# A twelve-stage decoder on one core: layer norms by one-pass moments (BN_STATS, BN_AGGR), scaled and transposed sequence by sequence

## The reference

```python
def _layernorm(x, axis=-1, eps=1e-05):
    m = jnp.mean(x, axis=axis, keepdims=True)
    v = jnp.var(x, axis=axis, keepdims=True)
    return (x - m) / jnp.sqrt(v + eps)

x = x + _L0_attn_ref(_layernorm(x, axis=-1), ...)
x = x + _L0_xattn_ref(_layernorm(x, axis=-1), ...)
x = x + _L0_ffn_ref(_layernorm(x, axis=-1), ...)
...
x = x + _L3_ffn_ref(_layernorm(x, axis=-1), ...)
```

## Time and profile before

| | |
|---|---|
| median of 3 runs | 1576.84 us (1575.34 to 1582.71) |
| the profiled execution | 1576.1 us, of which the span from the first to the last instruction is 1574.2 us |
| busy in the span | PE 1247.6 us (79%), DVE 902.8 us (57%), ACT 730.8 us (46%), POOL 325.2 us (21%) |
| mean granted TensorE clock | 0.857 of full speed |

### The profile page before, as it was taken

How to read it: one execution, slowest core, us unless ns; L and a number is a source line. 1 busy time by engine, 2 the same in 40 slices (tenths; PEclk the granted TensorE clock), 3 DMA queues, 4 the chain that set the end, 5 groups by cost and what they waited for, 6 DMA issues and landing times. The chain is left out here.

```text
span 1574.2 us, 24800 instructions
## 1 busy us (share of the span) xinstructions
PE 1247.6 (79%) x9007; PEld 814.7 (52%) x9008; DVE 902.8 (57%) x1989; ACT 730.8 (46%) x1316; POOL 325.2 (21%) x360
## 2 busy tenths in 40 slices
PE   5999797357697997487776874769789979797998
PEld 2788364136455564144653651755544434364776
DVE  3688473765666445686678568445634455474211
ACT  2344363341265323477568554436566633363442
POOL 0222200003220002346356251022000034300000
PEclk9899698565788997786997997688989989598999
DMA  6000000020000000000000000015036910000000
GB/s 262 1 1 0 1 2 1 0 83 1 0 1 2 0 1 1 0 1 1 1 1 1 1 1 1 2 72 228 2 78 124 202 31 1 0 2 2 1 1 14
DMA packets 15200, 44.28 MB, mean 28 GB/s; under 512 B 1872, under 2 KB 4976, under 8 KB 14448
## 3 DMA queue, kind: packets, MB, share of 16 engines
q1 hardware_dynamic: 15088, 42.80, 9.4%
HBM read 42.01 MB, written 0.79 MB: 27 GB/s over the span
## 5 line engine op out<-in xcount | busy, mean ns | idle before, releaser
L745 DVE TENSOR_REDUCE L_xattn_top<-banks 128x4 f32<-128x512 f32 x128 | 80.6, 671 | 54.9 <-PE banks L603 54.9
L750 DVE TENSOR_TENSOR L_xattn_p<-banks,L_xattn_top 128x512 f32<-128x512 f32 x128 | 82.5, 686 | 4.8
L700 ACT ACTIVATE L_xattn_p<-L_xattn_p 128x512 f32<-128x512 f32 x128 | 75.8, 630 | 18.1 <-DVE L_xattn_p L750 18.1
L708 ACT ACTIVATE L_xattn_pT<-banks 128x512 f32<-128x512 f32 x128 | 69.7, 595 | 20.1 <-PE banks L616 20.1
L603 PE MATMUL banks<-L_xattn_ks,L_xattn_qT 32*128 32x512 f32 x256 | 76.6, 702 | 1.6 <-ACT L_xattn_qT L689 1.6
L492 PE MATMUL banks<-w_const,h 128*128 128x128 f32 x96 | 24.0, 407 | 66.1 <-DVE h L487 66.1
L1277 DVE TENSOR_TENSOR L_ffn_a<-L_ffn_a,L_ffn_share 128x512 f32<-128x512 f32 x64 | 39.9, 687 | 60.1 <-DMA L_ffn_share<-L_ffn_shares 57.6
L616 PE MATMUL banks<-w_const,L_xattn_p 128*128 128x128 f32 x512 | 69.5, 278 | 5.2 <-ACT L_xattn_p L700 5.2
L476 POOL MEMSET norm_power<- 128x8 f32 x12 | 1.3, 105 | 344.7 <-POOLq L79 322.7
L1189 PE MATMUL banks<-L_ffn_a,region_a 128*128 128x512 f32 x136 | 67.5, 601 | 5.2 <-DVE L_ffn_a L1277 5.2
L1520 ACT ACTIVATE L_ffn_aT<-banks,L_ffn_shift 128x512 f32<-128x512 f32 x64 | 43.3, 687 | 58.9 <-PE banks L1470 57.3
(11 more groups left out here) (518 smaller groups left out, 3187.2 us busy)
## 6 DMA issues: line engine op xcount, KB each, us to landing
L_ffn_share<-L_ffn_shares SPq DMA_DIRECT2D x32, 512.0 KB, 10.2
region_b<-in_L_ffn SPq DMA_DIRECT2D x1, 6216.0 KB, 29.8
region_a<-in_L_ffn SPq DMA_DIRECT2D x1, 4416.0 KB, 14.6
region_b<-in_L_attn SPq DMA_DIRECT2D x1, 3150.5 KB, 10.2
region_a<-in_L_ffn SPq DMA_DIRECT2D x1, 3080.5 KB, 21.8
region_b<-in_L_attn SPq DMA_DIRECT2D x1, 1633.5 KB, 10.5
region_b<-in_L_xattn SPq DMA_DIRECT2D x1, 835.0 KB, 11.3
w_tables<-in_tables SPq DMA_DIRECT2D x1, 832.0 KB, 14.2
```

What stands on the lines that cost most here:

```text
L700: nc.scalar.activation(p[:, m % 4, :], p[:, m % 4, :], ACT.Exp, scale=scale).then_inc(exped, 1)
L708: nc.scalar.activation(pT[:, n % 2, 2 * (P % 2) + e, :], tps[e][:], ACT.Copy).then_inc(pT_kept, 1)
L745: nc.vector.tensor_reduce(top[:, i, :], rows_of(score[i][:], 4), X, ALU.max)
L750: nc.vector.tensor_tensor(rows_of(p[:, i, :], 4), rows_of(score[i][:], 4), bc(top[:, i, :], 2, T), ALU.subtract).then_inc(centered, 1)
```

## The change

`Norm` is rewritten; the calls around it follow.

- `center` and `variance` become one step, `take_moments`: four BN_STATS, one per sequence, each reading 128 elements per partition and writing six; a drain; four BN_AGGR, each reading those six and writing the mean and the variance; a drain; one addition of 1e-5 over the four variances.
- `square` is gone from ACT, and with it the tile of squares.
- `scale` reads `x` again and subtracts the mean and multiplies by the reciprocal root in one TENSOR_SCALAR per sequence, with both as per-partition scalars. Each adds one to `h_ready`.
- `turn` waits once per sequence instead of once per half.
- The constant -0.5 is written once at the program's start instead of once per stage.

DVE's instructions per norm go from 12 to 26, ACT's from 4 to 2. Everything else, the order of the calls and all other waits, stays.

```diff
-    def center(self, dve, half):
-        nc, g, b = self.nc, self.g, slice(4 * half, 4 * half + 4)
-        nc.vector.tensor_reduce(self.total[:, b], g.x[:, b, :], X, ALU.add)
-        dve.drain()
-        nc.vector.tensor_scalar(self.mean[:, b], self.total[:, b], 1.0 / D, None, ALU.mult)
-        dve.drain()
-        nc.vector.tensor_tensor(g.h[:, b, :], g.x[:, b, :], bc(self.mean[:, b], 2, D),
-                                ALU.subtract).then_inc(self.centered, 1)
-
-    def square(self, act, half):
+    def take_moments(self, dve, half, eps=1e-5):
+        nc, g = self.nc, self.g
+        for n in range(4 * half, 4 * half + 4):
+            nc.vector.bn_stats(self.stats[:, n, :], g.x[:, n, :])
+        dve.drain()
+        for n in range(4 * half, 4 * half + 4):
+            nc.vector.bn_aggr(self.moments[:, n, :], self.stats[:, n, :])
+        dve.drain()
         b = slice(4 * half, 4 * half + 4)
-        act.wait_ge(self.centered, half + 1)
-        self.nc.scalar.activation(self.sq[:, b, :], self.g.h[:, b, :], ACT.Square).then_inc(self.squared, 1)
-
-    def variance(self, dve, half, eps=1e-5):
-        nc, b = self.nc, slice(4 * half, 4 * half + 4)
-        dve.wait_ge(self.squared, half + 1)
-        nc.vector.tensor_reduce(self.sumsq[:, b], self.sq[:, b, :], X, ALU.add)
-        dve.drain()
-        nc.vector.tensor_scalar(self.var[:, b], self.sumsq[:, b], 1.0 / D, eps, ALU.mult, ALU.add).then_inc(self.var_ready, 1)
-
-    def set_power(self, pool):
-        self.nc.gpsimd.memset(self.power[:], -0.5).then_inc(self.power_set, 1)
+        nc.vector.tensor_scalar(self.var[:, b], self.moments[:, b, 1], eps, None, ALU.add).then_inc(self.var_ready, 1)
 
     def invert(self, pool, half):
         b = slice(4 * half, 4 * half + 4)
-        pool.wait_ge(self.power_set, 1)
         pool.wait_ge(self.var_ready, half + 1)
...
     def scale(self, dve, half):
-        nc, g, b = self.nc, self.g, slice(4 * half, 4 * half + 4)
+        nc, g = self.nc, self.g
         dve.wait_ge(self.rstd_ready, half + 1)
-        nc.vector.tensor_tensor(g.h[:, b, :], g.h[:, b, :], bc(self.rstd[:, b], 2, D), ALU.mult).then_inc(self.h_ready, 1)
+        for n in range(4 * half, 4 * half + 4):
+            nc.vector.tensor_scalar(g.h[:, n, :], g.x[:, n, :], self.moments[:, n, 0:1], self.rstd[:, n:n + 1],
+                                    ALU.subtract, ALU.mult).then_inc(self.h_ready, 1)
 
     def turn(self, pe, half, bank):
-        pe.wait_ge(self.h_ready, half + 1)
         for j in range(4):
+            pe.wait_ge(self.h_ready, 4 * half + j + 1)
             last = self.nc.tensor.transpose(bank[:, j * T:(j + 1) * T], self.g.h[:, 4 * half + j, :], self.g.ident)
         last.then_inc(self.turned, 1)
```

More of the change, by code:

```diff
@@ L127, in _ @@
             for half in range(2):
-                norm.center(dve, half)
-            for half in range(2):
-                norm.variance(dve, half)
+                norm.take_moments(dve, half)
             for half in range(2):
@@ L135, in _ @@
         def _(pool):
-            norm.set_power(pool)
             for half in range(2):
@@ L146, in _ @@
         def _(act):
-            for half in range(2):
-                norm.square(act, half)
             for half in range(2):
@@ L203, in _ @@
                 nc.gpsimd.memset(g.ones_slots[:], 0.0)
+                nc.gpsimd.memset(g.norm_scratch[4][:], -0.5)
                 pool.drain()
@@ L714, in keep_raw @@
                 nc.scalar.activation(raw[:, n % 2, :, :], rows_of(mix[n % 2][:, 0:2 * T], 2), ACT.Copy).then_inc(raw_kept, 1)
-            norm.square(act, 0)
-            norm.square(act, 1)
             if not keys_here:
@@ L768, in add @@
                 nc.vector.tensor_tensor(g.x[:, n, :], g.x[:, n, :], mix_part(n, PROJECTED), ALU.add).then_inc(added, 1)
-            norm.center(dve, 0)
-            norm.center(dve, 1)
-            norm.variance(dve, 0)
-            norm.variance(dve, 1)
+            norm.take_moments(dve, 0)
+            norm.take_moments(dve, 1)
             norm.scale(dve, 0)
@@ L3290, in build @@
     g.mask_loaded = nc.alloc_semaphore("mask_loaded")
-    g.norm_scratch = [sb(f"norm_{n}", [T, B] + [D] * (n == "squares"), F32)
-                      for n in ("total", "mean", "squares", "sumsq", "var", "rstd", "power")]
+    g.norm_scratch = [sb("norm_stats", [T, B, 6], F32), sb("norm_moments", [T, B, 2], F32)] + [
+        sb(f"norm_{n}", [T, B], F32) for n in ("var", "rstd", "power")]
     x_loaded, stored = nc.alloc_semaphore("x_loaded"), nc.alloc_semaphore("stored")
```

8 lines of the change are left out of this document (3 added, 5 removed).

## The result

The changed kernel takes 1534.35 us, the median of four runs (1533.25 to 1534.92), against 1576.17 us (1575.34 to 1582.71) for the kernel before, whose median here is over four runs instead of three: a ratio of 0.9729, with a 95% interval of 0.9706 to 0.9753. **The prediction was wrong in size**, right in sign.

What follows compares the result with a forecast made beforehand. The norm's chain through DVE, ACT, POOL and PE was taken to bind, paid twelve times. Stage gains 9.2 + 7.8 + 3.3 + 3.6 + 2.0 + 0.4 = 26.3 us gave a median of 1550.5 us, range 1543 to 1564.

Steps and rivals of the forecast that it cites:

- the length of the norm: In all twelve norms, the shorter chain brings the copies to hT earlier, 26.3 us in sum.
- Prices: In each norm on DVE: BN_STATS 0.29 us, BN_AGGR 0.17, one scaling of 128 elements 0.29.
- the rival of full lengths: DVE's BN and scaling instructions don't overlap: gain 16 us, 1561; chance 0.21 together with upper prices.
- the rule of the count of operations: The skill's advice to minimise DVE operations, each followed by a flush; 12 become 26 per norm, giving 1561.
- The exclusion of power and scaling: Rival: POOL's power and DVE's scaling take turns, 0.7 us later in four stages, 2.8 in sum, 1553.3; chance 0.12.
- Slower: Rival: dearer BN_STATS and BN_AGGR ahead of both scalings, 0.55 and 0.36 us each, give 1590; chance 0.05.
- the second memset of `values`: In the cross-attentions, it may hold scale(1) for 1.9 us, but PE asks for that half 5 us later: covered.
- the clock: Rival: PE's clock steps fall elsewhere; 1570 at mean 0.844, other way under 1543; chances 0.07 giving back, 0.05 adding.
- the clock adding to the gain: The clock rival's favourable side, a higher mean clock for PE: under 1543 us; chance 0.05.

Runs made afterwards that it cites:

- e3: The changed kernel with, in the four cross-attentions, POOL's two powers ahead of the memsets of values and the memsets held until all eight sequences are scaled: 1529.00 us.
- e6: The kernel before with only the scaling and the transposes per sequence; sums, squares and variances as before: 1588.17 us.
- e2: The changed kernel with three spare DVE instructions, some 2.3 us together, ahead of the first scaling in L1_xattn and L2_xattn alone: 1549.77 us.
- e9: The changed kernel with two spare DVE instructions at the head of the first norm only, a start 1.5 us later: 1543.23 us.
- e12: The kernel before with four spare DVE instructions at the head of the first norm only, a start 3.1 us later: 1579.24 us.
- e5: The kernel before with BN_STATS and BN_AGGR for the moments, but centring, scaling and transposing by whole halves as before: 1548.62 us.

## Why the prediction was wrong, and where it was right

**Right: the length of the norm.** The copies come 26.6 us earlier in sum, against 26.3. Prices: BN_STATS and BN_AGGR within 0.02 us of those taken; the scaling 0.05 dearer, hidden under PE's 0.25 us per transpose. The overlap of DVE's instructions, taken from the earlier trace rows, holds for the new kinds too, so the rival of full lengths falls, and with it the rule of the count of operations: DVE's instructions went from 1989 to 2157 and its busy time from 902.8 to 892.1 us. The exclusion of power and scaling falls by the timeline above. "Slower" falls with the prices.

**Right in sum, off by place.** L0_xattn gave 3.7 instead of 3.3. The first addition ended with the memset as forecast (2.06 us after the norm's start), but half 1's BN_STATS had begun beside it while it was held and took 1.05 us for four, so half 1's variance was ready at 3.25 instead of 3.7. L3_attn gave 2.4 instead of 2.0. L1_xattn gave 2.7 instead of 1.8: I let its values' products end as before, but they took 1.25 us instead of 1.91 at the higher clock.

**Wrong: the second memset of `values`.** The prediction put it beside `scale(1)`, "so it is covered". Where the powers run back to back, the memset begins 0.9 us after the first scaling of half 0, and the fourth scaling begins 0.8 us after the first, just ahead of it. The step set the memset against a half that is one instruction, as before, and not against its fourth part. In L3_xattn the copy lost 1.4 us instead of gaining 0.4, and the stage fell back to the lower clock as before. e3, which also starts the powers 1.9 us earlier, shows 9.6 us for both in that stage. e6 shows the same collision in all four cross-attentions, in a kernel that lost 12 us.

**Wrong, and the cause of the miss: the clock.** "The norm's gaps get shorter, so I lean to neither." The rival that held the outcome, the clock adding to the gain, had a chance of 0.05, and the sum had nothing for it. A gap that gets shorter is a reason to lean. PE's stops in L1_xattn (1.80 us) and L2_xattn (2.23) end altogether, and the products of the next 8 us had run at 0.59 and 0.50. I read the earlier trace rows for the copy alone and never asked at which clock the work behind it ran. The two stages gave 8.1 us beyond their copies; e2 takes them away again, and e9 to e12 show that they come with the change at every start tried. In all stages PE's products behind the copies took 11.6 us less. The mean clock was no price for it: by the prediction's own sum a mean of 0.871 instead of 0.857 would be 20 us of PE's time, and PE's busy time fell by 8.0.

**Partly open.** Of the other 7 us of the 15, 1.4 are the start of the first norm. The rest comes and goes with a shift of the start, so it belongs to the placement in time, and that the first measurement had it is luck. What in L0_attn, L2_ffn or L3_attn decides at which moment the clock rises or falls was not found, nor whether in the two cross-attentions it is PE's stop or the lateness behind it. The trace of before could have bounded the term: behind the two norms the clock stood at the lower level for 10.2 and 13.7 us, of which at most half, 12 us, was to be had. That is an estimate made afterwards; with it the forecast would have been 1538 to 1550, still above 1534.

## What to carry to other kernels

Ask of every gap that a change shortens or ends on the matrix engine at which granted clock the products behind it run; if it is the lower level, ending the gap may give back more than its length: here 1 us of lateness in front of such products was worth 2.5 to 4 us. Look for what a faster chain now meets on the shared parts: here a memset that no one had waited for fell on the scaling, and one part of the change by itself made the kernel slower. And where a shift of the start by 1.5 us moves the time by 9, the gain of one edit is known only to a few us unless both kernels are timed under several starts.

## What was not expected of the hardware

- **BN_STATS and BN_AGGR are cheap.** 128 fp32 elements per partition took 0.28 us at the median, one every 0.20 in a run of four; an aggregate of six values took 0.15.
- **A memset of POOL can hold a DVE TENSOR_SCALAR whose recorded start is earlier.** In L3_xattn the addition L458 began at 1313.18, the memset at 1313.29, and the addition ended with the memset, after 2.05 us instead of 0.17. The Trainium skill (SBUF — State Buffer, "Who interferes with whom") says that whoever issues first gets the shared ports for the whole instruction; the traces agree with the exclusion, and with the order from a recorded lead of 0.13 us on: a scaling that started 0.12 us or less ahead of the memset was held for all four memsets in a row, and one with 0.13 or more got through (19 cases, above, and one of each kind at 0.124). BN_STATS beside the same kind of memset kept its length in L1_xattn (0.88 us for four).
- **A TENSOR_TENSOR of DVE delays a power of POOL if it began first.** In e5 DVE begins to subtract 512 elements 0.17 us ahead of most powers, and these take 1.38 us instead of 1.01. In before a TENSOR_TENSOR of the same size begins 0.06 us behind a power, and the power keeps its 1.01. A TENSOR_SCALAR of 128 elements that began 0.17 us ahead, in the changed kernel, left it at 1.03. The mean of all 24 powers of e5 is 1285 ns, against 1021 in the changed kernel (from its groups by shape):

```profile
L464 POOL TENSOR_TENSOR norm_rstd<-norm_var,norm_power 128x4 f32<-128x4 f32 x24 | 30.8, 1285 | 193.4 <-DVE norm_var L458 193.2
```
